# A cross-attention loop: the key projection put between transposes and products, maxima and normalisation in two halves

## The reference, cut to what matters

```python
Q = (query @ w_q.T).reshape(b, sq, NUM_HEADS, D_K).transpose(0, 2, 1, 3)
K = (key @ w_k.T).reshape(b, sk, NUM_HEADS, D_K).transpose(0, 2, 1, 3)
V = (value @ w_v.T).reshape(b, sk, NUM_HEADS, D_K).transpose(0, 2, 1, 3)
scores = jnp.einsum('bhqd,bhkd->bhqk', Q, K) / scale
scores = scores + _alibi_bias(sq, sk, scores.dtype)[None]
attn = jax.nn.softmax(scores, axis=-1)
ctx = jnp.einsum('bhqk,bhkd->bqhd', attn, V).reshape(b, sq, D_MODEL)
return ctx @ w_o.T + b_o
```

## Time and profile before

| | |
|---|---|
| median of three runs | 1930.89 us (1924.9 to 1931.84) |
| the profiled execution's own time | 1929.83 us |
| its span, first to last instruction | 1928.2 us |
| mean granted PE clock over the span | 0.902 of full speed |
| PE busy over the span | 1672.4 us, 87% |
| DVE, ACT, POOL busy | 1059.2, 755.5, 746.0 us |
| the touched loop | about 47 to 291 us of the span |

### The profile page before, as it was taken

How to read it: one execution, slowest core, us unless ns; L and a number is a source line. 1 busy time by engine, 2 the same in 40 slices (tenths; PEclk the granted TensorE clock), 3 DMA queues, 4 the chain that set the end, 5 groups by cost and what they waited for, 6 DMA issues and landing times.

```text
span 1928.2 us, 24024 instructions
## 1 busy us (share of the span) xinstructions
PE 1672.4 (87%) x8816; PEld 806.3 (42%) x8816; DVE 1059.2 (55%) x1548; ACT 755.5 (39%) x1191; POOL 746.0 (39%) x452
## 2 busy tenths in 40 slices
PE   7888886886999999999997769999803979899998
PEld 4666663541222232222224525444401557644443
DVE  2444444465998998998993333222368464422121
ACT  1333332275776776776771222111414240122121
POOL 0433331238998998998993010000000023000000
PEclk8999997788999999999999668999855879699999
DMA  2111101003000100100102400111071100100110
GB/s 68 33 33 33 33 27 53 0 14 104 8 19 7 28 16 8 30 13 8 31 5 67 176 0 1 49 33 33 15 168 39 33 0 1 45 9 35 44 44 22
DMA packets 37895, 66.64 MB, mean 35 GB/s; under 512 B 13764, under 2 KB 24408, under 8 KB 36260
## 3 DMA queue, kind: packets, MB, share of 16 engines
q1 hardware_dynamic: 34612, 64.47, 11.3%
q10 hardware_dynamic: 3200, 1.07, 0.2%
HBM read 56.33 MB, written 9.20 MB: 34 GB/s over the span
## 4 chain that ended last, share of the span: by engine, by line
PE 51%; POOL 22%; DVE 12%; issue 11%; DMA 2%; ACT 2%; SPq 1%; DVEq 0%; ACTq 0%; POOLq 0%
POOL arena L1247 20%; PE ps L1467 6%; PE ps L2203 6%; PE ps L2214 6%; PE ps L201 3%; PE ps L1480 3%; PE ps L342 3%; PE ps L347 3%; PE ps L224 3%; PE ps L360 2%; DVE arena L477 2%; PE ps L1978 2%; PE ps L1994 2%; DVE arena L488 1%; PE ps L217 1%
## 5 line engine op out<-in xcount | busy, mean ns | idle before, releaser
L1247 POOL TENSOR_TENSOR arena<-arena 128x768 f32<-128x768 f32 x248 | 532.4, 2187 | 23.2 <-DVE arena L1164 23.2
L867 PE MATMUL ps<-arena 32*128 32x512 f32 x1520 | 316.7, 653 | 0.9 <-ACT arena L1052 0.9
L1167 DVE TENSOR_TENSOR arena<-arena,ps 128x1024 f32<-128x1024 f32 x248 | 302.1, 1218 | 10.2 <-POOL arena L1247 5.5
L2160 POOL TENSOR_TENSOR arena<-arena 128x1024 f32<-128x1024 f32 x16 | 30.0, 1896 | 433.3 <-DVE arena L2093 418.6
L1045 ACT ACTIVATE arena<-arena 128x1024 f32<-128x1024 f32 x124 | 131.1, 1057 | 136.3 <-DVE arena L1147 136.3
L1147 DVE TENSOR_TENSOR arena<-arena,ps 128x1024 f32<-128x1024 f32 x124 | 151.4, 1221 | 22.0 <-PE ps L878 9.5
L915 PE MATMUL ps<-arena 128*32 128x512 f32 (+15 forms) x1024 | 136.9, 607 | 10.4 <-DVE arena L1167 9.9
L1052 ACT ACTIVATE arena<-ps 128x1024 f32<-128x1024 f32 x124 | 127.0, 1024 | 24.8 <-PE ps L867 9.7
L1054 ACT ACTIVATE arena<-arena 128x1024 f32<-128x1024 f32 x124 | 131.1, 1057 | 3.9
L1467 PE MATMUL ps<-arena 128*128 128x512 f32 x288 | 131.9, 602 | 0.5 <-ACT arena L1532 0.5
L867 PEld LDWEIGHTS ps<-arena 32*128 32x128 f32 x1520 | 103.3, 186 | 65.3 <-issue 58.6
(11 more groups left out here) (306 smaller groups left out, 2400.6 us busy)
## 6 DMA issues: line engine op xcount, KB each, us to landing
arena<-ctxT SPq DMA_DIRECT2D x32, 257.0 KB, 3.0
arena<-ctxT SPq DMA_DIRECT2D x8, 1028.0 KB, 15.7
arena<-L_ffn_w SPq DMA_DIRECT2D x16, 512.0 KB, 4.3
arena<-ctx_rows SPq DMA_DIRECT2D x8, 960.0 KB
arena<-L_ffn_eW SPq DMA_DIRECT2D x8, 512.0 KB, 3.7
m_rows<-arena SPq DMA_DIRECT2D x12, 256.0 KB, 2.8
arena<-m_rows SPq DMA_DIRECT2D x32, 64.0 KB
m_yd<-arena SPq DMA_DIRECT2D x64, 32.0 KB, 2.3
```

The costliest lines, as they stand in the source:

```text
L867: mm = nc.tensor.matmul(ps[:, bank + jj, :], weights[r], m_row[r, n // CH % 2, n % CH, :], start=start, stop=True)
L1167: nc.vector.tensor_tensor(m_h[:, u, n % 2], m_xa[:, u, n % 2], ps[:, bank:bank + 2, :], ALU.add).then_inc(S["m_use"], 1)
L1247: nc.gpsimd.tensor_tensor(x, x, m_h[:, u, (n - 1) % 2].rearrange("p j d -> p (j d)")[:, own], ALU.mult).then_inc(S["m_kept"], 1)
```

## The change

- **Row 257's key** is projected ahead of the loop for all items, together with its value (8 more matmul records after the 8 of L329), copied by DVE into `kl`, and put by POOL into the last column of the key tile, one small copy for each item in `qblk`. The key projection in the loop then has 256 columns instead of 257, and fits for both feature blocks into one bank.
- **Banks**: keys go to bank 6, values to bank 4, transposes to banks 4 and 5 as before.
- **Order on PE**: scores of b+1, transposes of b (`turn`), keys of b+2, products of b (`weigh`), values of b+2.
- **Order on ACT**: block copy of b, exponentials of b+1, keys copy of b+2. **On DVE**: maxima of b+1, block copy of b, inverse sums of b+1, outputs of b, values copy of b+2.
- **Halves**: the scores signal after each pair of groups; maxima and their negation are two instructions each for half the groups, and the exponentials wait for each half; the scores of a pair of groups wait for the earlier item's exponentials of that pair alone. The normalisation is two instructions, one for each block of 128 columns, and each block's transposes wait for their own.

```diff
-            for m in range(DC):
-                for k in range(DC):
-                    mm = nc.tensor.matmul(ps[:, 0, m * B:(m + 1) * B], x0["wv"][:, k, m * P:(m + 1) * P],
-                                          x0["cl"][:, k, :], start=(k == 0), stop=(k == 1))
+            for n, w in enumerate((x0["wv"], x0["wk"])):
+                for m in range(DC):
+                    o = (DC * n + m) * B
+                    for k in range(DC):
+                        mm = nc.tensor.matmul(ps[:, 0, o:o + B], w[:, k, m * P:(m + 1) * P],
+                                              x0["cl"][:, k, :], start=(k == 0), stop=(k == 1))
...
+            def keys(b, j, i):
+                pe.wait_ge(*S.at(f"x_ctx{j}", 16 * (i + 1)))
+                if not isinstance(b, int) or b >= 1:
+                    pe.wait_ge(*S.at("x_kev", b))
+                for m in range(DC):
+                    for k in range(DC):
+                        mm = nc.tensor.matmul(ps[:, 6, m * (SK - 1):(m + 1) * (SK - 1)], x0["wk"][:, k, m * P:(m + 1) * P],
+                                              x0["ctx"][j][:, k, 0:SK - 1], start=(k == 0), stop=(k == 1))
+                mm.then_inc(S["x_k"], 1)
+
+            def values(b, j):
                 if not isinstance(b, int) or b >= 1:
                     pe.wait_ge(*S.at("x_vev", b))
...
-                        mm = nc.tensor.matmul(ps[:, 6, t * D:(t + 1) * D], cx[:, k, t * P:(t + 1) * P],
+                        mm = nc.tensor.matmul(ps[:, 4, t * D:(t + 1) * D], x0["ctx"][j][:, k, t * P:(t + 1) * P],
...
                 pe.wait_ge(*S.at("x_kev", b + 1))
-                pe.wait_ge(*S.at("x_qblk", 2 * b + 2))
-                if not isinstance(b, int) or b >= 1:
-                    pe.wait_ge(*S.at("x_exp", 4 * b))
+                pe.wait_ge(*S.at("x_qblk", 3 * b + 3))
                 for c in range(DC):
+                    if not isinstance(b, int) or b >= 1:
+                        pe.wait_ge(*S.at("x_exp", 4 * b - 2 + 2 * c))
...
-            def tail(b, j):
-
-
-                pe.wait_ge(*S.at("x_norm", b + 1))
+            def turn(b, j):
+                pe.wait_ge(*S.at("x_vev", min(b + 2, B) if isinstance(b, int) else b + 2))
                 for t in range(2):
+                    pe.wait_ge(*S.at("x_norm", 2 * b + 1 + t))
...
+            def weigh(b, j):
                 pe.wait_ge(*S.at("x_or", b + 1))
...
             with pe.Fori(0, B // 2 - 1) as i:
-                b = 2 * i
-                proj(b + 1, 1, i)
-                scores(b + 1, 1)
-                tail(b, 0)
-                proj(b + 2, 0, i + 1)
-                scores(b + 2, 0)
-                tail(b + 1, 1)
+                for j in range(2):
+                    b = 2 * i + j
+                    scores(b + 1, 1 - j)
+                    turn(b, j)
+                    keys(b + 2, j, i + 1)
+                    weigh(b, j)
+                    values(b + 2, j)
...
+                for j in range(2):
+                    b = 2 * i + j
+                    turned(b)
+                    exps(b + 1, 1 - j)
+                    keys(b + 2, j)
...
             def maxima(b, j):
-                dve.wait_ge(*S.at("x_s", b + 1))
-                nc.vector.tensor_reduce(x0["st"][j][:, 2, :], ps[:, 0:4, 0:SK], AX.X, ALU.max).then_inc(S["x_mx0"], 1)
...
+                for c in range(DC):
+                    own = slice(2 * c, 2 * c + 2)
+                    dve.wait_ge(*S.at("x_s", 2 * b + c + 1))
+                    nc.vector.tensor_reduce(x0["st"][j][:, 2, own], ps[:, own, 0:SK], AX.X, ALU.max).then_inc(S["x_mx0"], 1)
...
+                for j in range(2):
+                    b = 2 * i + j
+                    maxima(b + 1, 1 - j)
+                    turned(b)
+                    sums(b + 1, 1 - j)
+                    outs(b)
+                    values(b + 2, j)
...
+                nc.gpsimd.tensor_copy(x0["kT"][j][:, :, SK - 1:SK], x0["kl"][:, :, bass.ds(b, 1)]).then_inc(S["x_qblk"], 1)
...
-                nc.gpsimd.tensor_tensor(x0["p"][j][:, :, 0:SK - 1], x0["p"][j][:, :, 0:SK - 1],
-                                        x0["st"][j][:, 2, :].unsqueeze(2).broadcast_to([P, 4, SK - 1]),
-                                        ALU.mult).then_inc(S["x_norm"], 1)
-
+                for t in range(2):
+                    own = slice(t * P, (t + 1) * P)
+                    nc.gpsimd.tensor_tensor(x0["p"][j][:, :, own], x0["p"][j][:, :, own],
+                                            x0["st"][j][:, 2, :].unsqueeze(2).broadcast_to([P, 4, P]),
+                                            ALU.mult).then_inc(S["x_norm"], 1)
+
+            pool.wait_ge(*S.at("x_vlast", 1))
             qblk(0, 0)
```

More of the change, by code:

```diff
@@ L386, in tail @@
                 mm.then_inc(S["x_o"], 1)
-            proj(0, 0, 0)
+            keys(0, 0, 0)
+            values(0, 0)
             pe.wait_ge(*S.at("x_alibi", 4))
             scores(0, 0)
+            keys(1, 1, 0)
+            values(1, 1)
             with pe.Fori(0, B // 2 - 1) as i:
-                b = 2 * i
-                proj(b + 1, 1, i)
-                scores(b + 1, 1)
-                tail(b, 0)
-                proj(b + 2, 0, i + 1)
-                scores(b + 2, 0)
-                tail(b + 1, 1)
-            proj(B - 1, 1, B // 2 - 1)
+                for j in range(2):
[5 more added lines that the diff above has]
+                    values(b + 2, j)
             scores(B - 1, 1)
-            tail(B - 2, 0)
-            tail(B - 1, 1)
+            turn(B - 2, 0)
+            weigh(B - 2, 0)
+            turn(B - 1, 1)
+            weigh(B - 1, 1)
             pe.wait_ge(*S.at("x_or", B + 1))
@@ L423, in keys @@
                 act.wait_ge(*S.at("x_k", b + 1))
-                nc.scalar.copy(x0["kT"][j], ps[:, 4:6, 0:SK]).then_inc(S["x_kev"], 1)
+                nc.scalar.copy(x0["kT"][j][:, :, 0:SK - 1],
+                               ps[:, 6, :].rearrange("p (m s) -> p m s", m=DC)).then_inc(S["x_kev"], 1)
             def exps(b, j):
-                act.wait_ge(*S.at("x_max", b + 1))
                 for g in range(4):
+                    if g % 2 == 0:
+                        act.wait_ge(*S.at("x_max", 2 * b + 1 + g // 2))
                     nc.scalar.activation(x0["p"][j][:, g, :], ps[:, g, 0:SK], ACT.Exp,
@@ L439, in x_act @@
             exps(0, 0)
+            keys(1, 1)
             with act.Fori(0, B // 2 - 1) as i:
[L441 to L448, removed]
+                for j in range(2):
[3 more added lines that the diff above has]
+                    keys(b + 2, j)
             turned(B - 2)
@@ L465, in x_dve @@
             ch.link(nc.vector.tensor_reduce(x0["par"], hmask.rearrange("p (a i) -> p i a", i=2), AX.X, ALU.add))
-            nc.vector.tensor_copy(x0["vl"].rearrange("p c b -> p (c b)"), ps[:, 0, 0:DC * B]).then_inc(S["x_vlast"], 1)
+            nc.vector.tensor_copy(x0["vkl"], ps[:, 0, 0:2 * DC * B]).then_inc(S["x_vlast"], 1)
             for r in (slice(0, 6), slice(64, 70)):
@@ L472, in values @@
                 dve.wait_ge(*S.at("x_v", b + 1))
-                nc.vector.tensor_copy(x0["v"][j].rearrange("p a b -> p (a b)"), ps[:, 6, :]).then_inc(S["x_vev"], 1)
+                nc.vector.tensor_copy(x0["v"][j].rearrange("p a b -> p (a b)"), ps[:, 4, :]).then_inc(S["x_vev"], 1)
             def maxima(b, j):
-                dve.wait_ge(*S.at("x_s", b + 1))
-                nc.vector.tensor_reduce(x0["st"][j][:, 2, :], ps[:, 0:4, 0:SK], AX.X, ALU.max).then_inc(S["x_mx0"], 1)
-                dve.wait_ge(*S.at("x_mx0", b + 1))
-                nc.vector.tensor_scalar(x0["st"][j][:, 0, :], x0["st"][j][:, 2, :], -1.0, None,
-                                        ALU.mult).then_inc(S["x_max"], 1)
+                for c in range(DC):
+                    own = slice(2 * c, 2 * c + 2)
+                    dve.wait_ge(*S.at("x_s", 2 * b + c + 1))
+                    nc.vector.tensor_reduce(x0["st"][j][:, 2, own], ps[:, own, 0:SK], AX.X, ALU.max).then_inc(S["x_mx0"], 1)
+                    dve.wait_ge(*S.at("x_mx0", 2 * b + c + 1))
+                    nc.vector.tensor_scalar(x0["st"][j][:, 0, own], x0["st"][j][:, 2, own], -1.0, None,
+                                            ALU.mult).then_inc(S["x_max"], 1)
             def sums(b, j):
@@ L484, in sums, with turned, outs @@
                 nc.vector.reciprocal(x0["st"][j][:, 2, :], x0["st"][j][:, 1, :]).then_inc(S["x_rec"], 1)
-            def outs(b):
+            def turned(b):
                 dve.wait_ge(*S.at("x_pt", 2 * b + 2))
                 nc.vector.tensor_copy(x0["pT"][:, 1, :], ps[:, 5, :]).then_inc(S["x_pt1ev"], 1)
+            def outs(b):
                 dve.wait_ge(*S.at("x_o", b + 1))
@@ L501, in x_dve @@
             sums(0, 0)
+            values(1, 1)
             with dve.Fori(0, B // 2 - 1) as i:
[L503 to L512, removed]
+                for j in range(2):
[5 more added lines that the diff above has]
+                    values(b + 2, j)
```

(8 more changed lines are left out.)

15 lines of the change are left out of this document (3 added, 12 removed).

## The result

| | before | changed |
|---|---|---|
| median | 1931.19 us (4 runs, 1924.9 to 1931.84) | 1897.1 us (4 runs, 1893.27 to 1899.2) |
| profiled execution: time, span | 1929.83, 1928.2 us | 1899.2, 1897.6 us |
| scores to scores in the loop | 8.137 us | 6.958 us |

The ratio is 0.9828, with a 95% interval of 0.9802 to 0.9855: 34 us less, where 31 were forecast. A second measurement gave 0.9819 (0.98 to 0.9838).

The account below looks back on a forecast made before the run. PE was taken to bound the loop, with two short stalls per item. 30 x (8.137 - 7.10) - 0.5 = 30.6 us saved, so 1899.2 profiled and 1900 us for the median; range 1893 to 1914.

Parts of the forecast that it names:

- PE's own sum: In the loop, the start-to-start steps of PE's six groups of work add to 7.01 us per item.
- the joints: Transposes to keys, keys to products, products to values on PE: new successions, bounded 6.95 to 7.47 us per item, taken 7.10.
- Both stalls covered: In each item, PE's waits for ACT's and DVE's block copies vanish, with margins of 1.4 and 0.9 us.
- The margin of 0.9: In each item, DVE's copy of block 1 ends at 3.54 us, 0.9 before the products need it.
- The halves gain nothing on the path: Splitting the maxima in the loop gains nothing, since ACT copies its block first; it costs DVE 0.3 us per item.
- The edge hidden: At the loop's edge, 0.17 us per item of issue wait disappears behind the values; if it stays, 1905 us, chance 0.22.
- The shift ahead of the loop: Ahead of the loop, eight more short PE records delay item 1's scores by 0.3 to 0.9 us, taken as 0.5.
- The profiled execution's 1899.2: Whole kernel: profiled time of 1929.83 less a 30.6 us gain gives 1899.2 us; main forecast's chance 0.62.
- Nothing behind the loop: From the last item's scores to the spreading L519, the 7.57 us stay the same; everything later is untouched.
- The ring through ACT: Loop rival: scores, transposes, ACT's copy, exponentials, keys copy bind; 6.0 us by the rows, 7.7 if late, 1918 us, chance 0.07.
- Nor did issue: Loop rival: PE's instruction issue, 60 ns each, sets the time; item 8.59 us, kernel slower at 1945 us, chance 0.04.
- No gain: Loop rival: a 1.0 us wait returns elsewhere, nearest at transposes behind DVE's values copy; item 8.1 us, 1931 us, chance 0.05.

Follow-up runs that it names:

- the last experiment: Kernel before with only the 8 more short matmul records ahead of the loop, their results used by nothing; 1930.72 us, ratio 1.0003.

## Why the prediction was right, step by step

- **PE's own sum, 7.01, and 7.10 with the joints.** Right, and 0.14 too high. Measured 6.96. Scores took 1.69 for 1.70, transposes 0.93 for 0.95 and keys 1.83 for 1.82. The products took 0.58 for 0.72 and the values behind them 1.93 for 1.82, together 2.51 for 2.54; why the one is shorter and the other longer is not shown. The three new joints cost nothing, the lower end of their bounds. Reckoning from start to start instead of by the idle time was what made it fit: the listed idle was 25.1 us of 236, some 26 us over the loop, and 35.4 were saved; most of the difference is the end of transposes and products before each wait, which is counted as busy.
- **Both stalls covered.** Shown twice: undone in order, ACT's stall returns and the item costs 0.63 more; made late by 1.56 us, DVE's copy stalls PE again. The margin of 0.9 was 1.1. The prediction counted it to the first of the products; those that read block 1 start 0.36 later by its own rows, which makes it 1.3.
- **The halves gain nothing on the path.** Shown: 6.959 without them. The prediction did not say what they would be worth alone, 11 us.
- **The edge hidden.** Right, and not isolated: no "issue" before PE's matmuls in the changed kernel nor in the one with products behind, and it is still there, 0.38 for a pass, in the kernel with the old order. That the values at the end hide it is argued. The Trainium skill ("TensorE: Matmul & The Clock Gate", architectural detail) gives TensorE a queue of 64 instructions from which weight loads are pulled ahead. The missing edge fits that, but no run here measures the queue. The values that the prediction calls 16 records are 8 records and their 8 loads.
- **The shift ahead of the loop, 0.5.** Mis-sized: 2.3. The records started 0.32 later, cost their 0.92 (the last experiment has 0.89), and 0.57 came back since PE no longer waits for ACT's keys before item 1's scores: 0.67 without the clock, inside the 0.3 to 0.9. What was left out is the clock. The first keys ran at the lower level of 1.2 GHz, 3.47 us to the next group instead of 1.82. It took back 1.65 of the 4.3 us that the loop gave beyond the forecast.
- **The profiled execution's 1899.2, forecast to the digit.** Luck: the loop gave 4.3 more and the stretch behind it 0.2, the stretch ahead took 1.8 more, and 2.6 went in untouched stages, which about cancels.
- **Nothing behind the loop.** 0.23, expected 0.
- **The rivals.** The ring through ACT did not bind: the loop ran at 6.33 with PE's bias work gone. Nor did issue: an item has 6.958 / 136 = 51 ns for each record and load, and within it the 32 records of the products and their 32 loads take 0.58 us, 9 ns each; the waits added in the new order cost nothing. "No gain" fell with the time.

## What to carry to other kernels

Where two groups of work on the bound engine pass through a copy on another engine, put an independent group between them, at least as long as the copy with its queue; here one line of order was worth 18 us, and shortening what stood ahead of the copy was worth 11 alone and nothing beside it. Price a reordering by the steps from start to start of each group, not by the idle time, which here understated the gain by a quarter. When the waits are gone, count the bound engine's own instructions again: moving four bias matmuls to an engine at half load was worth another 11 us, 14.5 in the loop less what their setup cost ahead of it.

## What the runs showed that I had not expected

- The scores of an item alternate two float32 matmuls and two bf16 bias matmuls of 6 rows, twice. Without the bias pairs the whole takes 1.07 us from start to start instead of 1.69: 0.31 for a pair whose own step was 0.21.
- The clock ahead of the loop differs between executions of kernels that are alike up to there: 2.0 or 3.6 us for the same 8 records, and the start of the 16 short ones anywhere from 33.7 to 37.2 us. In the nine profiles with the keys directly behind them, the slow ones are those whose clock had risen latest before the records.
- A stall can settle on every second item: with the bias on DVE items took 6.33 and 6.62 us by turns, and the count of waits alone (26) did not tell this from a wait in every item.
